# A transformer layer with routed experts on one core: hidden unit 8p + c of the first expert layer moves to partition p, so that w2 loads in 8 KB rows

## The reference, cut to what matters

```python
logits = x @ router_w.T + router_b + 0.1 * expert_weights   # x is normalised
top_p, top_i = top_k(softmax(logits), 2);  top_p /= top_p.sum()
h = gelu(einsum('bsd,edh->bseh', x, w1) + b1)               # w1: 8 x 256 x 1024
expert_out = einsum('bseh,ehd->bsed', h, w2) + b2           # w2: 8 x 1024 x 256
out = x + (top_p * expert_out[chosen]).sum(over the two)
```

## Time and profile before

| what | value |
|---|---|
| median of 3 runs | 729.85 us (726.82 to 731.17) |
| the profiled execution's own time | 732.77 us |
| its span | 730.8 us |
| mean granted TensorE clock | 0.973 of full |
| busy share: PE, DVE, ACT, POOL | 91%, 48%, 55%, 39% |
| moved by DMA | 78.29 MB, 62240 packets |

### The profile page before, as it was taken

The page is one execution under the profiler, slowest core; times in us unless marked ns, Lnnn a source line. Parts: engine busy times, 40 slices in busy tenths (PEclk is TensorE's granted clock), DMA queues, the critical chain, the costliest instruction groups (busy, mean ns, idle before and its releaser), DMA issues.

```text
span 730.8 us, 15649 instructions
## 1 busy us (share of the span) xinstructions
PE 664.7 (91%) x5027; PEld 519.3 (71%) x5027; DVE 351.2 (48%) x812; ACT 405.5 (55%) x880; POOL 287.8 (39%) x543
## 2 busy tenths in 40 slices
PE   7679999999999999899864999899999999999996
PEld 4445666766667666566542488788999999999995
DVE  2397787776868777768832434411212222121211
ACT  4444657575776777667433665553454544545451
POOL 3233345153442454643272263633424242434322
PEclk9899999999999999989977999999999999999999
DMA  5545445456445555754799552142222222212121
GB/s 132 144 126 159 132 114 173 138 157 173 138 137 155 166 142 148 241 166 131 204 149 174 160 152 52 23 38 39 33 42 36 38 37 37 39 35 44 31 30 22
DMA packets 62240, 78.29 MB, mean 107 GB/s; under 512 B 14446, under 2 KB 52721, under 8 KB 62161
## 3 DMA queue, kind: packets, MB, share of 16 engines
q1 hardware_dynamic: 48841, 62.42, 32.5%
q0 software_dynamic: 8512, 10.26, 9.4%
q10 hardware_dynamic: 4808, 4.61, 2.0%
HBM read 54.52 MB, written 22.35 MB: 105 GB/s over the span
## 4 chain that ended last, share of the span: by engine, by line
PE 66%; SPq 8%; issue 6%; DVE 6%; POOL 5%; ACT 4%; DMA 4%; another core or an unknown queue 0%; ACTq 0%; DVEq 0%; POOLq 0%
PE attention_psum L740 18%; PE attention_psum L747 17%; PE attention_psum L732 6%; PE attention_psum L689 5%; PE attention_psum L704 4%; PE attention_psum L780 4%; PE attention_psum L638 3%; PE attention_psum L644 3%; SPq L586 2%; SPq L571 2%; DMA weights<-maxT 2%; PE attention_psum L633 2%; SPq L564 2%; DVE neg_max L1222 1%; PE attention_psum L818 1%
## 5 line engine op out<-in xcount | busy, mean ns | idle before, releaser
L912 ACT ACTIVATE weights<-attention_psum 128x512 f32<-128x512 f32 x256 | 147.4, 596 | 93.4 <-PE attention_psum L704 81.8
L1222 DVE TENSOR_REDUCE neg_max<-attention_psum 128x2 f32<-128x512 f32 x256 | 168.4, 684 | 51.4 <-PE attention_psum L689 42.0
L740 PE MATMUL attention_psum<-over,v 128*128 128x128 f32 x1248 | 146.4, 275 | 0.0
L747 PE MATMUL attention_psum<-weights 128*128 x624 | 142.8, 380 | 1.9 <-issue 1.8
L740 PEld LDWEIGHTS attention_psum<-over,v 128*128 128x128 f32 x1248 | 143.1, 192 | 0.2
L1006 ACT ACTIVATE weights<-attention_psum,b_sb 128x128 f32<-128x128 f32 x312 | 89.5, 370 | 85.4 <-PE attention_psum L740 71.9
L1486 POOL DMA_INDIRECT out<-over x39 | 63.0, 1616 | 168.8 <-DVE over L1280 160.0
L747 PEld LDWEIGHTS attention_psum<-weights 128*128 128x128 f32 x624 | 115.5, 190 | 17.7 <-issue 3.7
L689 PE MATMUL attention_psum<-weights 99*128 99x256 bf16 x512 | 100.0, 277 | 12.8 <-DVE neg_max L1222 11.9
L1274 DVE TENSOR_TENSOR over<-attention_psum,b_sb 128x256 f32<-128x256 f32 x39 | 16.6, 425 | 197.5 <-PE attention_psum L747 196.2
L704 PE MATMUL attention_psum<-weights 102*128 102x256 bf16 x512 | 99.2, 277 | 13.2 <-DMA weights<-maxT 12.1
(11 more groups left out here) (166 smaller groups left out, 743.9 us busy)
## 6 DMA issues: line engine op xcount, KB each, us to landing
parts<-weights SPq DMA_DIRECT2D x96, 128.0 KB
weights<-parts SPq DMA_DIRECT2D x64, 192.0 KB
weights<-parts SPq DMA_DIRECT2D x64, 128.0 KB
weights<-in_L_ffn_w SPq DMA_DIRECT2D x8, 1024.0 KB
weights<-parts SPq DMA_DIRECT2D x64, 64.0 KB
w_sb<-in_L_ffn_w SPq DMA_DIRECT2D x8, 512.0 KB
weights<-in_L_ffn_w SPq DMA_DIRECT2D x8, 512.0 KB
weights<-in_x SPq DMA_DIRECT2D x8, 256.0 KB, 3.3
```

The lines of the kernel that those rows point to most:

```text
L740: last = pe.matmul(m.hT_bank[j % 2][:, c * P:(c + 1) * P], m.w1t[j % 2][:, k, c * P:(c + 1) * P], m.xT[j % 2][:, k, :], start=(k == 0), st ...
L747: last = pe.matmul(m.bank_of(("down_a", TILE, j))[:, 0:D], m.hidT[j % HIDDEN][:, c, :], m.w2_sb[:, bass.ds(expert, 1), c, :].rearrange("p ...
L912: act.activation(m.p[:, u % P_RING, :], m.b_bank[u % B_RING], ACT.Exp, scale=SCALE[ORDER[u // H][0]]).then_inc(m.b_free[u % B_RING], 1)
L1222: v.tensor_reduce(m.neg_max[:, :, h:h + 1], m.a_bank[u % A_RING].rearrange("p (t k) -> p t k", t=T), AXX, ALU.max, negate=True).then_inc(m ...
```

## The change

Hidden unit 8p + c now lies on partition p, in group c, everywhere:

```diff
-sp.dma_start(m.b1_in[:, :], b1.rearrange("e (c p) -> (e c) p", p=P)).then_inc(m.s_b, 16)
+sp.dma_start(m.b1_sb[:, :, :], b1.rearrange("e (p c) -> p e c", c=FC)).then_inc(m.s_b, 16)
...
-sp.dma_start(m.w2_sb[:, n, :, :], w2[n].rearrange("(c p) d -> p c d", p=P)).then_inc(m.s_w2, 16)
+sp.dma_start(m.w2_sb[:, n, :, :], w2[n].rearrange("(p c) d -> p c d", c=FC)).then_inc(m.s_w2, 16)
...
-act.copy(m.w1t[n % 2][:, 0, :], m.w1_sb[0][:, bass.ds(e, 1), :].rearrange("p a n -> p (a n)")
+act.copy(m.w1t[n % 2][:, 0, :].rearrange("p (c q) -> p c q", c=FC),
+         m.w1_sb[0][:, bass.ds(e, 1), :].rearrange("p a (q c) -> p (a c) q", c=FC)
...
-v.tensor_copy(m.w1t[n % 2][:, 1, :], m.w1_sb[1][:, bass.ds(e, 1), :].rearrange("p a n -> p (a n)")
+v.tensor_copy(m.w1t[n % 2][:, 1, :].rearrange("p (c q) -> p c q", c=FC),
+              m.w1_sb[1][:, bass.ds(e, 1), :].rearrange("p a (q c) -> p (a c) q", c=FC)
...
-slots[12 * H + 12].pieces.append(("b1", SELF, 0))
-            elif name == "b1":
-                pe.wait_ge(m.s_b, 16)
-                pe.transpose(fill(piece)[:, 0:E * FC], m.b1_in[:, :],
-                             m.ident[0:E * FC, 0:E * FC]).then_inc(m.fills(piece), 1)
...
-            elif name == "b1":
-                v.wait_ge(*m.filled(piece))
-                v.tensor_copy(m.b1_sb[:, :, :].rearrange("p e c -> p (e c)"),
-                              m.bank_of(piece)[:, 0:E * FC]).then_inc(m.frees(piece), 1)
...
-                        act.wait_ge(*m.emptied(("b1", SELF, 0)))
+                        act.wait_ge(m.s_b, 16)
```

More of the change, by code:

```diff
@@ L273, in schedule @@
     return [slots[at] for at in range(first, last)]
-RING = ("turn", "qk", "v", "stack", "max", "ot", "cturn", "proj", "rturn", "logits", "b1", "count", "counted",
+RING = ("turn", "qk", "v", "stack", "max", "ot", "cturn", "proj", "rturn", "logits", "count", "counted",
         "xturn", "down_a")
@@ L340, in shared @@
         self.entry = sb("entry", [P, TOPK, NT, 2])
-        self.b1_in, self.b1_sb, self.b2_sb = sb("b1_in", [E * FC, P]), sb("b1_sb", [P, E, FC]), sb("b2_sb", [P, E, D])
+        self.b1_sb, self.b2_sb = sb("b1_sb", [P, E, FC]), sb("b2_sb", [P, E, D])
     def for_attention(self):
```

## The result

The changed kernel is slower. The first comparison gave 736.88 us (734.87 to 740.85, 4 runs) beside 729.35 us for the kernel before (726.82 to 731.17, 4 runs), a ratio of 1.0099 with a 95% interval of 1.0067 to 1.0131. A later one gave 1.0060 (1.0035 to 1.0085). The forecast was 725.5 us, so it had the wrong sign, and the time lies outside its range of 718.5 to 733. Ratios are to the kernel before, with a 95% interval in brackets.

A forecast was written before the change was run, and what follows sets the result against it. TensorE was taken to bound the tiles, and its 9.16 us wait for row maxima to be shortenable. Terms -6.1 (w2), -0.3 and +1.0 (b1), +1.0 (copies) gave -4.4: 725.5 us from 729.85, range 718.5 to 733.

The forecast's parts named there:

- w2 in 8 KB rows: Last attention units, 363 to 401 us: larger w2 pieces shorten TensorE's 9.16 us wait for row maxima; -6.1 us.
- the rate: w2's loads from 363 to 401 us: larger pieces move 7% more per busy DMA time, landing the maxima earlier; -2.1 us.
- the line: Same stretch: DMA engines ran dry behind SP's queue full of 1024-piece loads; 128 pieces win that idle time back; -4.0 us.
- the landing is set by something else: Rival, 363 to 401 us: list writes slow HBM, so 5 MB need 38 us whatever the pieces; +1.7, 731.5 us; chance 0.22.
- The rival that came nearest in time: List writes fall behind 8 KB pieces on the DMA engines, delaying the first gathers; +6.5, 736.4 us; chance 0.13.
- The turn's 0.3 us: TensorE's turn of b1, in the chain of waits, falls away; -0.3 us.
- the load's +1.0: b1's load on SP becomes 1024 pieces of 32 B and delays row maxima issued there; +1.0 us, bounds 0 and +3.5.
- The mark I named for it: Sign that the b1 term is wrong: maxima at 305 us land more than 2 us later than before.
- The surcharge: w1 copies read in 32-byte steps: 0.58 ns more per element, 0.6 us on ACT's copy, the same on DVE's.
- The charge of +1.0 us at the end: ACT's w1 copies before the steady state: +0.5 us for two of three near the path; bounds 0 and +3.2.
- The doubling: Upper bound for ACT's w1 copy of 1.05 us, read in 32-byte steps: +1.05 us.

The follow-up runs named there:

- e3_w2_cut: Changed kernel with each expert's w2 loaded in two interleaving transfers, same row order in 1 KB packets: 1.0049 (1.0022 to 1.0075) on the kernel before.
- w2 undone: Changed kernel with w2 back in 1 KB rows, b1's direct load and the turned copies kept: 1.0000 (0.9972 to 1.0028) on the kernel before.
- e2_held: Changed kernel with w2's loads 1 to 3 issued behind the last unit's first maxima: 726.12 us, 0.9930 (0.9906 to 0.9953) on the kernel before.

## Why the prediction was wrong

*The step that failed* is "w2 in 8 KB rows", both its terms, -2.1 for the rate and -4.0 for the line, together -6.1 us. I read engines that ran dry (4.0 us of idle share) as the sign that SP's full queue set the landing. The full queue did go, as forecast, and the issues took 0.43 and 1.45 us. But it had not been the bound. The list writes were: without them the kernel before moved 367 GB/s in place of 169, and its stalls at issuing shrank to a third; with them, feeding the engines sooner raised the share to 0.93 to 0.98 and left the rate at 146 to 165 GB/s. Nor was it the place in line, since on ACT's queue the maxima held TensorE until 403.88 all the same. So the two terms were no gain. Measured, w2's rows alone gave 1.0023 in the jam, an interval from a gain of 0.6 us to a loss of 4.0, and +0.2 us out of it. The rate term's reading of the pieces was right in direction and too small: without list writes the window goes from 367 to 417 GB/s, 14% and not 7%. It was wrong in where it falls: it is not on the path.

*The right rival* was "the landing is set by something else": HBM or the engines slowed by the list writes. Its mark, a share of 0.92 at 155 GB/s, was on the table, and I gave it 0.22. A share near 1 at less than half the rate of the window behind it (315 at 0.97) meant packets that took longer, and no faster feeding shortens these. That rival's 731.5 us was below the measured time as well: it had no price for sending more into the jam. The rival that came nearest in time, 736.4 us, rests on the large packet, and `e3_w2_cut` was slower without it; its nearness to 736.88 is at least in part luck.

*b1.* The turn's 0.3 us and the load's +1.0 (bounds 0 to 3.5): 1.0000 alone, +0.7 us without the jam, neither told from zero. The term stands within what can be measured. The mark I named for it, that the maxima at 305 us land more than 2 us later, did come: TensorE resumes at 312.82 in place of 310.36, 2.46 us later. But it was no good one, since kernels with the same load range from 311.06 to 315.32 and those without it from 309.47 to 313.94. The means of these two groups are 1.5 us apart, which is near the term.

*The copies.* The surcharge was taken from one reduce with 16-byte steps: 0.6 us on ACT, against a measured 1.01; for DVE 0.6 against 0.41. The charge of +1.0 us at the end compares with +1.6 without the jam, neither told from zero nor from 1.0, and nothing that could be told with it. The doubling was my bound. TensorE stayed at 100 of 100 us, as forecast. The charge also counted three copies ahead of the steady state where ACT's order of time from 404 to 443 us has four: one at 436.78 us is not in the earlier trace rows.

*The sum.* Forecast -6.1 - 0.3 + 1.0 + 1.0 = -4.4. For b1 and the copies the forecast was +1.7, and the medians without the jam give +2.3. The whole is 734.96 - 730.93 = +4.0 in the larger comparison and +7.5 in the first. All parts together were +2.5 without the jam, so 1.5 us or more would be w2's loads in the jam, if the parts cost the same there. Against that stands w2 undone, where b1 and the copies together gave 1.0000; the split is an estimate within the noise. What exactly w2's loads do in the jam stays open. The profile shows SP no longer held back, so that three of w2's loads and two of w1's are issued by 368.3 us, where before SP stood in the two w1 issues until 371.2 and 379.3. That the earlier bytes make the jam longer would fit `e2_held`, the higher share and the later list reads, but w2 cut had SP held back for 5.19 us once more and was about as slow. No run held back the issue alone.

## What to carry to other kernels

A DMA share near 1 with a rate far below a neighbouring stretch was here no sign that the transfer needs larger pieces. Look for small writes to HBM in the same stretch, and leave them out once, to see what they cost. Then keep bulk loads out of their way: a load that nothing needs yet belongs behind the small transfer that an engine waits for, and another queue is no substitute for that order. A stall at issuing can be an effect of a slow stretch and not its cause, so ask of each one removed what then starts earlier and whom it meets.

## What the runs showed of the hardware

- 16 indirect writes of 128 entries of 8 bytes each, to HBM, were issued over 24 us. Leaving them out, with the wait for them, made the kernel before 2.5% faster (735.21 - 716.38 = 18.8 us). With them and the loads in their slots the DMA engines moved 146 to 177 GB/s from 363 to 401 us (nine traces). In the window from 368 to 373 us it was 169 GB/s with them and 367 without in the kernel before, 157 and 421 in the changed one. In the changed kernel the list writes of all batches landed 5.3 to 18.6 us after issue. The Trainium skill ("DMA: Bandwidth & Descriptors", Specifications) says that below 512 B the engine does a read-modify-write. The Trainium skill ("DMA: Bandwidth & Descriptors", Queues, rings and completion order) says that a semaphore's increment lands only after every earlier write of that engine, across its queues. The second fits what the maxima did on ACT's queue, and would let any small write delay any landing; no run here tells the two apart.
- The Trainium skill ("DMA: Bandwidth & Descriptors", Issuing engines are not separate DMA queues) says that another issuing engine saves only the time of issuing. The runs agree: 1.0078 against 1.0060, and TensorE stood for the first half's maxima until 403.88 us against 403.42 and 405.65.
- A read of fp32 from SBUF in steps of 32 bytes took 2061 ns instead of 1057 on ScalarE for 1024 elements a partition, 1099 instead of 694 on VectorE, and 335 instead of 192 for a 128x128 weight load of TensorE.
- Without the list writes, the window from 368 to 373 us moved 417 to 421 GB/s with w2 in 8 KB rows and 367 with 1 KB pieces, part of w1's 4 KB rows in each. 8 KB rows behind the list writes moved 426 at a share of 1.01, 1 KB pieces 315 at 0.97.
